# A graph layer's opening stage: load order, head statistics on TensorE, and scratch laid into the gather ring

## The reference, cut to what matters

```python
xn = _layernorm(x, axis=-1)
# mix: k and v are the rows of xn, split in heads of 32
def _layernorm(x, weight, bias):
    mean = jnp.mean(x, axis=-1, keepdims=True)
    std = jnp.std(x, axis=-1, keepdims=True, ddof=1)
    return weight * (x - mean) / (std + EPS) + bias
kv = jnp.einsum('bhnd,bhne->bhde', k, v) / N
out = jnp.einsum('bhnd,bhde->bhne', q, kv)
x = x + gnn(xn, edges) + out + xn
x = x + ffn(_layernorm(x))
```

## Time and profile before

| | us |
|---|---|
| device time, median of 3 runs | 1316.77 |
| device time, lowest and highest | 1305.88, 1317.27 |
| span of the profiled execution | 1163.6 |
| median of the runs less the span | 153.2 |

### The profile page before, as it was taken

The page is one execution under the profiler, slowest core; times in us unless marked ns, Lnnn a source line. Parts: engine busy times, 40 slices in busy tenths (PEclk is TensorE's granted clock), DMA queues, the critical chain, the costliest instruction groups (busy, mean ns, idle before and its releaser), DMA issues.

```text
span 1163.6 us, 27165 instructions
## 1 busy us (share of the span) xinstructions
PE 1056.7 (91%) x8001; PEld 1003.1 (86%) x8002; DVE 762.1 (65%) x1942; ACT 623.8 (54%) x1948; POOL 634.9 (55%) x700
## 2 busy tenths in 40 slices
PE   1377999999999999999998977799999999999993
PEld 1267999999999999999997975699999999999992
DVE  6888999999999999999984658333333333333330
ACT  3329555555555555555554760655555555555550
POOL 2474777777777777777731300444444444444431
PEclk9568999999999999999997989899999999999997
DMA  6532333333333333333320334583222222222224
GB/s 160 160 91 68 111 109 112 103 108 103 109 113 105 110 109 109 109 111 105 105 61 5 106 117 181 177 296 65 36 36 34 38 36 36 36 36 36 35 29 124
DMA packets 47378, 108.51 MB, mean 93 GB/s; under 512 B 13814, under 2 KB 24871, under 8 KB 45160
## 3 DMA queue, kind: packets, MB, share of 16 engines
q0 software_dynamic: 30720, 69.24, 24.2%
q1 hardware_dynamic: 16308, 37.47, 9.9%
q10 hardware_dynamic: 308, 1.28, 0.3%
HBM read 90.88 MB, written 20.27 MB: 96 GB/s over the span
## 4 chain that ended last, share of the span: by engine, by line
PE 44%; issue 15%; DVE 12%; POOL 10%; ACT 9%; DVEq 4%; DMA 4%; SPq 0%; POOLq 0%; ACTq 0%
PE ps L961 17%; PE ps L975 16%; POOL xg L556 10%; ACT e L1115 5%; DMA xg<-xn_rows,idx_st 3%; DVEq L1551 2%; PE ps L813 1%; PE ps L864 1%; DVE neg_top L1452 1%; PE ps L860 1%; PE ps L945 1%; ACT agg L1148 1%; PE ps L889 1%; PE ps L699 1%; PE ps L861 1%
## 5 line engine op out<-in xcount | busy, mean ns | idle before, releaser
L556 POOL DMA_INDIRECT xg<-xn_rows,idx_st x416 | 417.5, 1004 | 170.3 <-issue 124.6
L813 PE MATMUL ps<-sel,xg 128*128 128x120 f32 x2496 | 298.5, 276 | 3.8 <-DVE sel L1540 1.3
L813 PEld LDWEIGHTS ps<-sel,xg 128*128 128x128 f32 x2496 | 286.8, 192 | 10.0 <-issue 9.2
L1266 ACT ACTIVATE ht_sb<-ps,b_cur 128x128 f32<-128x128 f32 x448 | 127.9, 369 | 162.5 <-PE ps L961 162.5
L961 PEld LDWEIGHTS ps<-xst,w_st 128*128 128x128 f32 x1792 | 210.1, 193 | 5.6 <-issue 2.8
L961 PE MATMUL ps<-xst,w_st 128*128 128x128 f32 x1792 | 210.6, 276 | 2.3 <-ACT ht_sb L1266 1.7
L1115 ACT ACTIVATE e<-ps,neg_top 128x65 f32<-128x65 f32 x416 | 125.4, 316 | 161.8 <-DVE neg_top L1452 143.7
L975 PE MATMUL ps<-w_sb,ht_sb 128*128 x896 | 202.8, 379 | 0.8 <-DVE y_sb L1845 0.8
L626 POOL DMA_INDIRECT sum_rows<-y_sb,put_st x56 | 108.4, 1935 | 145.6 <-DVE y_sb L1848 135.4
L975 PEld LDWEIGHTS ps<-w_sb,ht_sb 128*128 128x128 f32 x896 | 166.7, 191 | 21.4 <-issue 1.2
L1845 DVE TENSOR_TENSOR y_sb<-ps,b_bc 128x256 f32<-128x256 f32 x56 | 23.8, 425 | 184.2 <-PE ps L975 184.2
(11 more groups left out here) (271 smaller groups left out, 1363.1 us busy)
## 6 DMA issues: line engine op xcount, KB each, us to landing
w_sb<-in_L_ffn_W SPq DMA_DIRECT2D x16, 1024.0 KB, 6.8
xg<-xn_rows,idx_st POOLq DMA_INDIRECT x416
x_sb<-in_x SPq DMA_DIRECT2D x5, 560.0 KB
xn_rows<-xn_sb SPq DMA_DIRECT2D x5, 560.0 KB
xn_t<-xn_rows SPq DMA_DIRECT2D x25, 112.0 KB
expert_in_rows<-xf_sb SPq DMA_DIRECT2D x12, 224.0 KB
sum_rows<-x_sb SPq DMA_DIRECT2D x12, 224.0 KB
out<-sum_rows SPq DMA_DIRECT2D x3, 560.0 KB
```

The costliest lines, as they stand in the source:

```text
L556: pool.indirect_dma_start(xg[:, s, tt, M:M + D], None, xn_dram, bass.IndirectOffsetOnAxis(ap=idx_st[:, s, tt:tt + 1], axis=0)).then_inc(ma ...
L813: mm = pe.matmul(ps3[:, s, col:col + n], xg[:, r, tt, lhs0:lhs0 + 128], sel[:, s, lo:lo + n], start=(tt == 0), stop=(tt == TG - 1))
L1266: ins = act.activation(ht_sb[:, o % 2, c, :], h_of(c), ACT.Gelu, bias=b1_cur[:, o % 2, c:c + 1])
```

## The change

- SP loads all five batches of `x` first and the edge tables behind them. DVE does the table work after the row statistics. ACT normalises two batches instead of three, and DVE three; DVE's table work stands ahead of its three batches.
- ACT copies the edge tables after its part of the rows, with three squares of 416 elements a partition in addition, which replace DVE's square and reduction (two additions remain on DVE). The gather indices are staged as soon as the third table is copied.
- The head phase goes by pairs of tiles. PE transposes the pair (4), ACT copies it (512 elements), PE multiplies it by a centring matrix `centre = I - block/32` (4), ACT squares the deviations and copies them to `hx` (512 elements each), and DVE sums the squares, and per four tiles forms the quotients in place. `heads` and `dev` go. The composed weights, the unit vectors and the flags are spread over the pairs. PE runs 12 spare matmuls ahead (`WARM`).
- The scratch of the composition and of the pairs lies in the ring's slots 6 to 9, so GpSimd waits for `sums_ready` ahead of group 6. The raw edge tables lie under the loop's own tiles instead of under the ring.
- In the main loop DVE's `maxima` no longer waits for `main.exp`, nor `messages` for `main.o0`.

```diff
-    ACT_NB = 3
+    ACT_NB = 2
+    SQUARES = 4
+    WARM = 12
...
-            load_x(0)
+            for b in range(NB):
+                load_x(b)
             sp.wait_ge(raw_padded, 2)
...
-            for b in range(1, NB):
-                load_x(b)
...
+                if isinstance(i, int) and i == 0 and o == LATE_SLOT:
+                    pool.wait_ge(sums_ready, 1)
...
+            def turn_pair(q):
+                ...
+                if q >= 2:
+                    pe.wait_ge(turned_copied, q - 1)
+                for t, j in enumerate(tiles):
+                    for h in range(2):
+                        mm = pe.transpose(turned_ps(q)[:, t, h, :], xn_sb[:, j, h * 128:(h + 1) * 128], ident[0:P, 0:P])
+                mm.then_inc(rows_turned, 1)
+            def centre_pair(q):
+                pe.wait_ge(turned_copied, q + 1)
+                if q >= 2:
+                    pe.wait_ge(head_dev, q - 1)
+                for t in range(len(PAIRS[q])):
+                    for h in range(2):
+                        mm = pe.matmul(centred_ps(q)[:, t, h * 128:(h + 1) * 128], xtt[:, q % 2, t, h, :], centre[:, :],
+                                       start=True, stop=True)
+                mm.then_inc(rows_centred, 1)
...
+            for k in range(WARM):
+                pe.matmul(ps1[:, 0, 384:512], ident[:, :], ident[:, :], start=True, stop=True)
             pe.wait_ge(edge_cols_taken, len(tables))
...
+            for q in range(NQ):
+                centre_pair(q)
+                turn_pair(q + 2)
+                if q in COMPOSED_AFTER:
+                    COMPOSED_AFTER[q]()
+                if q >= 5 and q % 2 == 1:
+                    if q == 5:
+                        pe.wait_ge(banks_cleared, 1)
+                    head_sums((q - 5) // 2)
...
-            act.wait_ge(edges_ready, 1)
+            act.wait_ge(edge_cols_taken, 3)
             for k in range(0, RING, HALF):
                 stage_idx(0, k)
...
+            for q in range(NQ):
+                copy_turned(q + 1)
+                squares(q)
+                deviations_out(q)
+                if q in COPIED_AFTER:
+                    COPIED_AFTER[q]()
+                if q >= 3 and q % 2 == 1:
+                    head_deviation((q - 3) // 2)
...
+            for f in range(NF + 1):
+                if f < NF:
+                    for q in FOURS[f]:
+                        mean_squares(q)
+                if f >= 1:
+                    quotients(f - 1)
+                if f < 3:
+                    edge_units(f)
+                if f == 4:
+                    upper_weights()
+                if f == 5:
+                    flags()
...
-                if not isinstance(i, int) or o >= 2:
-                    dve.wait_ge(main.exp, RING * i + o - 1)
                 maxima_of(s).then_inc(main.neg_top, 1)
...
-                dve.wait_ge(main.o0, RING * i + o + 1)
                 dve.wait_ge(main.exp, RING * i + o + 1)
```

## The result

The changed kernel took **1324.9 us** (median of 4 runs, 1322.1 to 1330.2), the kernel before 1313.7 in the same job (4 runs, 1305.9 to 1317.3): ratio 1.0097, 95% interval 1.0056 to 1.0138. Forecast were 1304.7. The profiled execution took 1322.13 us with a span of 1320.4. So 1.7 us lie around a span, not 153: the page shown ahead of the prediction belongs to an execution in which the kernel before took some 1165 us (1163.6 and 1.7), and the timed runs took 150 us more *inside* the span.

The account below looks back on a forecast made before the run. In the loop TensorE and gathers were nearly equal limits, so the head phase's end counted: 33.0 + 34.3 = 67.3 instead of 79.36, span 1163.6 to 1151.5, plus 153.2 gives 1304.7 us; range 1297 to 1315.

Parts of the forecast that it names:

- With the 153.2 that lay around it: Whole kernel: 153.2 us were taken to lie around the span, added to a span of 1151.5 to give 1304.7 us.
- cost nothing, cover some 2 us: Gathers beside the head phase: start at 37 us, first 40 end near 94; the new wait for the sums costs nothing.
- A shift passes to the end one for one: Head phase to kernel end: sums ready 12.1 us earlier, at 67.3 instead of 79.36, shorten the total by as much.
- Who holds the phase: Head phase: VectorE's 26.0 us set its length, TensorE holding it only at the lower clock; 34.3 us in all.
- PE has 12 instructions a pair: TensorE in the head phase: 2.8 us a pair at the lower clock, 1.5 at the upper, against VectorE's 2.0.
- The bound for the lower clock: Head phase with TensorE at the lower clock throughout: 44 us, of which 150 instructions at 0.23 make 34.8.
- Opening: Before the head phase: statistics end at 18.4, tables land at 21.7, first pair turned at 33.0 instead of 39.66, 6.7 us gained.
- rival A: Head phase: TensorE stays at the lower clock, phase 43 to 44 us, sums at 77.5, total 1314.8 us; chance 0.16.
- The 3.2 us for pairs at the lower clock: Head phase: four of 13 pairs at the lower clock add 4 x 0.8 us within the 34.3.
- Pause at the restart: Gather stream at the loop's start: its 11.33 us pause, ended by step 4's indices, stays but shortens to some 2 us.
- Rival C: Head phase: hand-offs don't overlap, 4.2 us a pair, sums at 90.6, 11.3 us slower, total 1328 us; chance 0.06.
- DVE waiting longer than it works: Sign in the changed profile's head phase that would show the hand-offs don't overlap; expected instead was VectorE busy for three quarters.

Follow-up runs that it names:

- e2: Changed kernel with the first gather held until the sums are ready; sums at 67.3 us, ratio 1.0187 against the kernel before (1302.8 us).
- e12: Changed kernel, unaltered, in a job where the kernel before took 1162.1 us: 1148.4 us, ratio 0.9882, sums at 69.1 us.
- e8: Changed kernel, unaltered, in a job where the kernel before took 1313.9 us: ratio 1.0055, sums at 93.1 us.
- e4: Kernel before with the new order of loads and of the opening alone, old head phase kept: ratio 1.0107 against the kernel before (1162.0 us).
- e3: Changed kernel without the 12 spare matmuls: ratio 1.0086 against the kernel before (1302.8 us), sums at 94.7 us.
- e11: Changed kernel with gathers held until the sums and 28 plain loads of 112 KB in the early gathers' place: ratio 1.0289 against the kernel before (1313.9 us).
- e16: Changed kernel whose first 24 gathers fetch half rows, beside a kernel before at 1300.8 us: one run, 1321.8 us, sums at 95.0 us.

## Why the prediction was wrong

- **The reading of the span: the first step that failed.** "With the 153.2 that lay around it": what lies around a span is 1.7 us. The 153 us were lost inside the span of the timed runs. The whole sum was made in one kind of job and carried as a shift to the other, where TensorE is held up. The table ahead of the prediction had the sign of it, and that a difference of 13% lies inside the span should have been a rival.
- **The gathers "cost nothing, cover some 2 us": the step that cost the time.** From 40 to 70 us TensorE gets 48, 8 and 6 instructions through in 10 us each, where it has 93 from 50 to 60 in e2, and the head phase took 60.3 us (32.7 to 93.0) instead of 34.3. With the gathers held it took 35.1 (32.2 to 67.3, e2). The length came out for a phase by itself and not for one with gathers beside it.
- **"A shift passes to the end one for one".** Without stops: the sums moved by 9.8 (78.9 to 69.1), step 4's indices by 9.9 (108.65 to 98.75), the median by 13.8 (e12); right within 4 us. (The sum's 79.36 is the end of `sum_diag`, its start is 78.87.) With stops: 93.1 against 78.9 is 14.2 later, the medians differ by 8.0 us (e8) and 11.1 (the result): not one for one.
- **Who holds the phase.** VectorE's sum was forecast at 26.0 and measured at 25.91. TensorE's was missed: "PE has 12 instructions a pair", but the trace has 50 transposes, 100 centring and 100 summing ones over 12.5 pairs, 20 a pair (fp32 products are recorded as two, which I counted for the old phase and not for the new one). At 33.35 / 286 = 0.117 us each that is 2.3 us a pair and not 1.5, so TensorE is busy for 93% of the phase at the upper clock, not for 60 to 70%. The bound for the lower clock rests on the same count: 150 x 0.23 = 34.8 would have been 250 x 0.23 = 57.5. That the length came out nearly right (34.3 against 35.1) is luck: 3.2 us of it were for a low clock that wasn't there. The count made the phase look as if it had a third of TensorE's time to spare, and a disturbance of TensorE wasn't among the rivals.
- **Opening.** Last statistics forecast to end at 18.4, measured 18.6; tables 21.7, measured 21.6; first pair 33.0, measured 32.7 and 34.0; first gather 37, measured 35.9 and 36.8. All held, the first pair by luck in part: the 38 instructions ahead of it were 50, since the 12 spare matmuls are recorded as 24, and the slow end was taken. The load order moves no sums by itself (e4), and the spare matmuls move them by 1.6 us (e3).
- **Clock (rival A).** It stood at 1.00 through the whole phase in e2, e11 and e12, with 4 of a pair's 20 instructions transposes. The rule of the Trainium skill ("TensorE: Matmul & The Clock Gate", Part 4) that transposes don't engage the full clock is not borne out for such a mix. The 3.2 us for pairs at the lower clock weren't needed in these three.
- **Pause at the restart.** "Shorter, some 2 us": 8.91 us (e12). The 40 gathers ended at 91.5 as forecast within 3 us (94), and the indices came at 98.75, not at 96.6; what ended the pause was a slot freed by TensorE.
- **Rival C** had the size (sums 90.6, total 1328) by luck, for its cause was another: it let each pair wait for the turn of the next. What came true of it is that the hand-offs got longer, since TensorE's signals were late (10.2 and 21.2 us for two pairs); and TensorE stood within a sum too, where no hand-off is. Its stated sign, "DVE waiting longer than it works", was there (VectorE is busy for 26.50 of 60.3 us), and it doesn't tell the two causes apart.

Shown: in a job with stops, it is the pace of the gathers beside the head phase, and not their bytes, plain loads at 72 GB/s or the spare matmuls, that makes the phase 26 us longer; and the changed kernel, 1.2% faster in a job without stops, is 0.6 to 1.0% slower in one with them. Open: why some jobs have the stops and others on the same chip have none; how much of TensorE's load a stop needs; and what holds TensorE. A lack of instructions alone doesn't explain it, since the signals of matmuls that are on record as ended come late as well. Each timed execution was recorded by the profiler, and no run shows whether the recording takes part.

## What to carry to other kernels

Compare the profiled execution's own time with its span before anything else: if the median of the runs is 13% above the span, the page and the timing are of two different conditions, and the forecast needs both. Count an engine's instructions by how the trace records them (here two for one fp32 product) before calling it unloaded. A wait put down to "issue" need not be one for nothing: look at what the instruction reads, who wrote it, and how long after its release that engine began. Here, work that moved from VectorE to TensorE came into the reach of GpSimd's gather stream; where the gathers are early and not urgent, letting them come 2.2 us apart, or in groups of four with pauses, while TensorE sets the pace kept the sums at 71.1 and 70.4, while holding them back wholly made the kernel 1.9% slower (e2).

## What was unexpected of the hardware

- In some jobs TensorE stands between instructions with nothing to wait for, while gathers of 128 rows are issued every 1.25 us: 0.3 to 1.8 us each in the kernel after, up to 2.42 in e16. In e16 many of these waits are 0.33, 1.03, 1.73 or 2.42 us, steps of 0.70. At one gather per 2.2 us, or with 72 GB/s of plain loads, there are none in the head phase.
- In the same jobs the signals of TensorE's matmuls come late, in the cases above 21 us (the kernel after) and 26 us (e2) after the matmuls' recorded ends, and the engines that wait for them stand meanwhile. In jobs without stops it is 0.02 us at most, up to the loop's end.
- The same kernel takes 1162 or 1301 us on the same chip in two jobs; 139 us of difference is ten times what the change is worth in either.
- TensorE's clock held 1.00 through a phase in which 50 of 286 instructions were transposes (e12).
